# Quantised attention: row maxima over two PSUM banks in one instruction, the tile's shift right behind them

## The reference, cut to what matters

```
q = _fq_sym(q, axis=-1); k = _fq_sym(k, axis=-1); v = _fq_sym(v, axis=2)
attn = jnp.einsum('bhqd,bhkd->bhqk', q, k)
attn = jax.nn.softmax(attn.astype(jnp.float32), axis=-1)
attn = _fq_unsigned(attn, axis=-1)      # s = max(row) / 255; round(x / s) clipped to 0..255, times s
out = jnp.einsum('bhqk,bhkd->bhqd', attn, v)
```

## Time and profile before

| what | value |
|---|---|
| median of 3 runs | 3547.64 us (3543.55 to 3548.8) |
| the profiled execution, its time | 3543.03 us |
| its span in the trace | 3541.3 us |
| the changed stage in it | about 938 to 1848 us |
| PE, DVE, ACT busy, share of the span | 77%, 73%, 52% |

### The profile page before, as it was taken

How to read it: one execution, slowest core, us unless ns; L and a number is a source line. 1 busy time by engine, 2 the same in 40 slices (tenths; PEclk the granted TensorE clock), 3 DMA queues, 4 the chain that set the end, 5 groups by cost and what they waited for, 6 DMA issues and landing times. The chain is left out here.

```text
span 3541.3 us, 63656 instructions
## 1 busy us (share of the span) xinstructions
PE 2737.0 (77%) x21394; PEld 1415.9 (40%) x21394; DVE 2572.9 (73%) x4720; ACT 1835.0 (52%) x2658; POOL 701.9 (20%) x577
## 2 busy tenths in 40 slices
PE   5925999785799999999986677786797547758983
PEld 3413444333365656565653333333111223224541
DVE  5555667566799999999984666524797787986547
ACT  2334433232499999999982433313676022434551
POOL 4422000012110101010104233203012503550012
PEclk8966999896899999999998788897998769978996
DMA  4251431200000000000001100100431000023301
GB/s 171 73 202 48 143 119 48 92 0 15 18 13 7 13 7 13 7 13 13 1 12 51 36 0 0 60 15 12 96 72 45 28 20 1 0 65 64 64 7 51
DMA packets 65283, 151.89 MB, mean 43 GB/s; under 512 B 11792, under 2 KB 20000, under 8 KB 63328
## 3 DMA queue, kind: packets, MB, share of 16 engines
q1 hardware_dynamic: 62320, 140.43, 13.1%
q0 software_dynamic: 2800, 9.18, 0.9%
HBM read 93.61 MB, written 24.38 MB: 33 GB/s over the span
## 5 line engine op out<-in xcount | busy, mean ns | idle before, releaser
L1507 DVE TENSOR_REDUCE s_top<-ps 128x1 f32<-128x512 f32 x1024 | 657.8, 685 | 32.8 <-PE ps L1402 32.3
L1476 ACT ACTIVATE s_prob<-ps,s_shift,m_sq 128x1024 int16<-128x1024 f32 x512 | 615.1, 1202 | 31.2 <-DVE s_shift L1515 31.2
L1402 PE MATMUL ps<-s_ks,s_qs 128*128 128x512 f16 x1024 | 352.4, 386 | 61.4 <-issue 15.3
L1407 PEld LDWEIGHTS ps<-ident,s_prob 128*128 128x128 f16 x4096 | 273.2, 98 | 123.3 <-DVE m_o L1525 52.1
L1407 PE MATMUL ps<-ident,s_prob 128*128 128x128 f16 x4096 | 314.6, 220 | 0.7 <-ACT s_prob L1476 0.5
L1395 PE MATMUL ps<-s_ks,s_qs 128*128 128x512 f16 x1024 | 307.2, 382 | 1.1 <-ACT s_prob L1476 0.5
L1482 ACT ACTIVATE s_probT<-ps 128x1024 f16<-128x1024 int16 x256 | 262.1, 1024 | 6.6 <-PE ps L1407 6.4
L246 PE MATMUL ps<-ident,s_parts 128*128 128x128 f16 x768 | 90.9, 291 | 165.9 <-POOL s_parts L237 164.2
L1520 DVE CAST s_probT<-ps 128x1024 f16<-128x1024 int16 x256 | 174.6, 682 | 3.0 <-PE ps L1407 2.9
L2166 DVE TENSOR_SCALAR s_prob<-ps,s_cap 128x1024 f32<-128x1024 f32 x128 | 158.2, 1271 | 25.2 <-PE ps L2075 25.2
L2747 DVE TENSOR_REDUCE s_ntop<-ps 128x1 f32<-128x512 f32 (+3 forms) x256 | 107.5, 484 | 86.6 <-PE ps L2607 86.6
(11 more groups left out here) (379 smaller groups left out, 5990.6 us busy)
## 6 DMA issues: line engine op xcount, KB each, us to landing
s_qs<-m_qT SPq DMA_DIRECT2D x144, 128.0 KB, 2.5
s_ks<-m_kT SPq DMA_DIRECT2D x96, 128.0 KB, 2.4
numbers<-s_numbers SPq DMA_DIRECT2D x21, 512.0 KB, 2.8
s_slabs<-numbers SPq DMA_DIRECT2D x21, 512.0 KB, 3.8
m_ks<-context_parts SPq DMA_DIRECT2D x12, 512.0 KB, 7.5
expert_rows<-s_y SPq DMA_DIRECT2D x19, 256.0 KB, 2.0
s_rows_in<-in_ctx SPq DMA_DIRECT2D x16, 256.0 KB, 3.0
x_sb<-in_x SPq DMA_DIRECT2D x1, 4096.0 KB, 14.2
```

Of the source, the lines that this page charges most:

```text
L1402: pe.matmul(quarter_at(q), qs[:, hb, bass.ds(t * P, P)], ks[:, hb, cols(q, 512)], start=True, stop=True).then_inc(s.top_scored, 1)
L1407: j = pe.transpose(turned(half, F16)[:, cols(m, P)], prob[:, u, cols(8 * half + m, P)].bitcast(F16), k.ident[:])
L1476: act.activation(prob[:, u, cols(half, HALF)], pair(half).rearrange("p m n -> p (m n)"), ACT.Exp, bias=shift[:, u:u + 1], scale=sq[:, bass ...
L1507: dve.tensor_reduce(top4[:, u, q:q + 1], quarter_at(q), AX.X, ALU.max).then_inc(s.top_read, 1)
```

## The change

Banks 4 and 5 become one buffer. PE waits once per half tile, until DVE has read the half before, and fills both banks with two matmuls, of which only the second one counts up `top_scored`. DVE takes the maximum of both banks, 1024 elements, in one reduce: two for a tile in place of four. The two results stand in `top2`. Behind the second one DVE waits for its result, takes the larger of the two (`ntop`), waits for that too, and makes the tile's shift at once, for tile n+2 where it was for tile n+1. Of DVE's steps for a tile `top_of` is gone as a separate step, and the rest keeps its order.

```diff
-            def score_for_top(n, quarters, hb, t):
-                for q in quarters:
-                    pe.wait_ge(s.top_read, 4 * n + q + 1)
-                    pe.matmul(quarter_at(q), qs[:, hb, bass.ds(t * P, P)], ks[:, hb, cols(q, 512)],
-                              start=True, stop=True).then_inc(s.top_scored, 1)
+            def score_for_top(n, half, hb, t):
+                pe.wait_ge(s.top_read, 2 * n + half + 1)
+                for m in range(2):
+                    j = pe.matmul(tops_at[:, m, :], qs[:, hb, bass.ds(t * P, P)], ks[:, hb, cols(2 * half + m, 512)],
+                                  start=True, stop=True)
+                j.then_inc(s.top_scored, 1)
...
-            def tops(n, u, quarters):
-                for q in quarters:
-                    dve.wait_ge(s.top_scored, 4 * n + q + 1)
-                    dve.tensor_reduce(top4[:, u, q:q + 1], quarter_at(q), AX.X, ALU.max).then_inc(s.top_read, 1)
-
-            def top_of(n, u):
-                dve.wait_ge(s.top_read, 4 * n + 4 + 2)
-                v.later(dve.tensor_reduce(ntop[:], top4[:, u, :], AX.X, ALU.max, negate=True))
+            def tops(n, u, half):
+                dve.wait_ge(s.top_scored, 2 * n + half + 1)
+                dve.tensor_reduce(top2[:, u, half:half + 1], tops_at.rearrange("p m n -> p (m n)"), AX.X, ALU.max
+                                  ).then_inc(s.top_read, 1)
 
             def shift_of(n, u):
-                v.catch_up()
+                dve.wait_ge(s.top_read, 2 * n + 3)
+                v.done(dve.tensor_reduce(ntop[:], top2[:, u, :], AX.X, ALU.max, negate=True))
                 dve.tensor_scalar(shift[:, u:u + 1], ntop[:], sq[:, bass.ds(n, 1)], LN255, ALU.mult,
                                   ALU.add).then_inc(s.shift_ready, 1)
...
                 if more:
-                    top_of(n + 1, (u + 1) % R)
-                if more == 2:
-                    tops(n + 2, (u + 2) % R, (0, 1))
-                if more:
-                    shift_of(n + 1, (u + 1) % R)
+                    tops(n + 2, (u + 2) % R, 0)
                 copy(n, u)
                 if not first:
                     evacuate(n - 1)
-                if more == 2:
-                    tops(n + 2, (u + 2) % R, (2, 3))
+                if more:
+                    tops(n + 2, (u + 2) % R, 1)
+                    shift_of(n + 2, (u + 2) % R)
```

More of the change, by code:

```diff
@@ L1335, in attention_quantised @@
         hv = s.sb("hv", [P, R, T, HD], F16)
-        top4 = s.sb("top4", [P, R, 4], F32)
+        top2 = s.sb("top2", [P, R, 2], F32)
         ntop = s.sb("ntop", [P, 1], F32)
@@ L1345, in pair @@
             return k.ps[:, 2 * half:2 * half + 2, :]
-        def quarter_at(q):
-            return k.ps[:, 4 + q % 2, :]
+        tops_at = k.ps[:, 4:6, :]
         def turned(half, dt):
@@ L1421, in tile @@
                 if next2 is not None:
-                    score_for_top(n + 2, (0, 1), *next2)
+                    score_for_top(n + 2, 0, *next2)
                 pe.wait_ge(s.exp_ready, 2 * n + 1)
@@ L1430, in tile @@
                 if next2 is not None:
-                    score_for_top(n + 2, (2, 3), *next2)
+                    score_for_top(n + 2, 1, *next2)
                 pe.wait_ge(s.exp_ready, 2 * n + 2)
@@ L1459, in _ @@
             pe.wait_ge(s.values_ready, 1)
-            score_for_top(0, range(4), 0, 0)
+            score_for_top(0, 0, 0, 0)
+            score_for_top(0, 1, 0, 0)
             score(0, 0, 0)
             score(1, 0, 0)
-            score_for_top(1, range(4), 0, 1)
+            score_for_top(1, 0, 0, 1)
+            score_for_top(1, 1, 0, 1)
             tile(0, 0, (0, 1), (0, 2))
@@ L1526, in evacuate, with tile @@
                                 output.unsqueeze(1)).then_inc(s.evacuated, 1)
-            def tile(n, u, first=False, more=2):
+            def tile(n, u, first=False, more=True):
                 if more:
-                    top_of(n + 1, (u + 1) % R)
-                if more == 2:
-                    tops(n + 2, (u + 2) % R, (0, 1))
-                if more:
-                    shift_of(n + 1, (u + 1) % R)
+                    tops(n + 2, (u + 2) % R, 0)
                 copy(n, u)
@@ L1538, in tile @@
                     evacuate(n - 1)
-                if more == 2:
-                    tops(n + 2, (u + 2) % R, (2, 3))
+                if more:
+                    tops(n + 2, (u + 2) % R, 1)
+                    shift_of(n + 2, (u + 2) % R)
             dve.nop().then_inc(s.half0_copied, 1)
             dve.nop().then_inc(s.evacuated, 1)
[L1544 to L1548, removed]
+            dve.nop().then_inc(s.top_read, 1)
+            for n in range(2):
+                tops(n, n, 0)
+                tops(n, n, 1)
+                shift_of(n, n)
             tile(0, 0, first=True)
@@ L1553, in _ @@
                     tile(2 * R * i + a + 2, (a + 2) % R)
-            tile(NT - 2, (NT - 2) % R, more=1)
-            tile(NT - 1, (NT - 1) % R, more=0)
+            tile(NT - 2, (NT - 2) % R, more=False)
+            tile(NT - 1, (NT - 1) % R, more=False)
             evacuate(NT - 1)
```

## The result

The changed kernel takes 3666.6 us (median of 4 runs, 3663.9 to 3671.86), the kernel before 3548.14 (4 runs, 3543.55 to 3548.8): a ratio of 1.034, 95% interval 1.0325 to 1.0355. It is 118 us slower.

The account below looks back on a forecast made before the run. DVE was taken to bound the kernel at 3.45 us a tile; two reduces of 1.22 us plus refills of 0.70 and 0.775 give 3.915, so 118 us more over 254 tiles: 3665 us, range 3635 to 3715.

Parts of the forecast that it names:

- a closed chain of two reduces and two refills: DVE and PE on banks 4 and 5: reduce, refill, reduce, refill without overlap set the tile at 3.915 us; 81 in 100.
- The bigger reduce: On DVE: a 1024-element reduce lasts 1.22 us and holds DVE 1.135, removing 0.13 us a tile.
- The refill: Between DVE's reduces: PE's wake-up, two matmuls and DVE's wake-up take 0.70 us, or 0.80 with a register-row wait.
- The prediction's list of signs: What the changed profile would show, including tiles of 3.83 us outside PE's inner loop and 3.93 inside.
- The shift is hidden: Behind a tile's second reduce: small reduce and shift take 0.35 to 0.47 us, shorter than the refill beside them.
- The sum: Per tile: two reduces and two refills make 3.915 us, 0.465 over 3.45; over 254 tiles 118 us more.
- PE stands ready: At each refill PE waits for DVE, with 0.14 us to spare at the second pair and 0.53 at the first.
- The rival of a late PE: At the second pair: PE 0.1 us late makes the tile 4.02 us, the kernel about 3690; 8 in 100.
- The rival of a falling clock: On PE: idle gaps lower the granted clock; one tile in four at the lower level gives 3779 us; 7 in 100.
- The refill hidden: On DVE: its own starts decide, at 3.40 to 3.52 us a tile, 3535 to 3565 us; 4 in 100.
- DVE waited 262 times: In the stage: DVE would wait for PE's scores some 250 times, where it waited 9 times.
- DVE's own work: On DVE: two bigger reduces take 2.27 us in place of 2.40, 0.13 us a tile less, 34 us in 254.

Follow-up runs that it names:

- e1: The changed kernel with its two-bank reduces kept and the shift put back where it was before: 3671.8 us, ratio 1.0366 to the kernel before.
- e2: The kernel before, with its four reduces, and only the shift moved right behind the last reduce: 3602.4 us against 3542.3, ratio 1.0175.
- e3: The changed kernel with PE scoring only the first of the two banks, one matmul per refill: 3594.4 us, ratio 1.0152 to the kernel before.
- e5: The kernel before with the small reduce moved behind the next tile's first bank reduce: 3522.1 us against 3544.0, ratio 0.9944.
- e7: The kernel of e2 with DVE's loop written out over 12 tiles in place of 6: 3593.3 us, ratio 1.014 to the kernel before.
- e6: The kernel of e2 with DVE's loop written out over 18 tiles in place of 6: 3628.5 us, ratio 1.0248 to the kernel before.

## Why the prediction was right

It gave 3665 us (3635 to 3715) and 118 us more; measured were 3666.6 and 118. The mechanism came as forecast, a closed chain of two reduces and two refills. That the number is right to 2 us is in part luck: between the two traces the stage grew by some 127 us, of which 5.5 lie ahead of the first copy, a stretch that the sum left at nothing; the runs of either kernel spread over 5 to 8 us.

- **The bigger reduce**, between rows 1.22 us: it is 1.225 (512 of them). It holds DVE for 1.14 until the next start, where 1.135 was worked out.
- **The refill**, 0.70 and 0.80 us from single links of the trace before: 0.71 and 0.80. That PE's wait in a register row makes the difference shows in the tiles: 3.95 inside PE's inner loop and 3.85 outside it. (The prediction's list of signs has 3.93 and 3.83; its own terms add up to 3.94 and 3.84.)
- **The shift is hidden**: e1 takes it away and wins nothing; e2 puts it where no refill hides it, and it costs 0.17 us a tile. It started 0.135 us behind the end of the small reduce, near the upper end of what was given.
- **The sum**: 3.915 us a tile was predicted, and 0.465 over before; the stage grew by 121.5 us in 255 distances, 0.477 each. The small excess, 3 us, is about what the rounds of DVE's loop cost: their tiles of 4.00 us are 0.05 over the others inside PE's inner loop and 0.15 over those outside it. The prediction had that in its upper end alone.
- **PE stands ready** at both pairs: its rows show 0.55 us of waiting ahead of the first and a start 0.07 us behind the reduce's end at the second. The rival of a late PE did not come.
- **The clock** stayed at 1.00 between the boundaries of groups of heads, with PE idle 0.55 us in each tile. The rival of a falling clock did not come. The page "TensorE: Matmul & The Clock Gate" of the Trainium skill, section "A second HAM failure mode: psum-queue depth-cycling", tells of a kernel whose short gaps between groups of matmuls did make the clock go down and up. No run here shows that for gaps of this length.
- **The refill hidden** was the rival of the other sign. e3 shows how far off it was: even with half a refill's matmuls the tile is 3.63, over the 3.45 of before.
- DVE waited 262 times (some 250 predicted), busy 89.37 of 100 (about 89).
- **DVE's own work** did get shorter, as forecast: 2 x 1.14 in place of 4 x 0.60 us, 0.12 a tile (0.13 predicted). With the buffer that the bigger reduces need, each tile still takes 0.48 us more. The page "Perfetto Trace Analysis" of the Trainium skill, section "Optimizing Scalar/DVE Operations", holds that larger operations can improve throughput if the engine is saturated. Here the engine was saturated and the measurement decides: the kernel is 3.4% slower. The fixed cost that this page of the Trainium skill states, and by which the prediction had an estimate of 0.25 us a tile, is about twice what these rows show.

## What to carry to other kernels

Where one engine fills and another empties the same banks, count buffers ahead of instructions: with two buffers of one bank DVE waited for the filling 9 times in the whole stage, with one buffer of two banks the tile became a closed chain of two reduces and two refills, each end of which is another engine's wake-up. Price such a chain link by link from the trace (end to load, load to matmul, matmul to next, end to start); each reduce and each refill came out within about 0.01 us of the sum's terms. What the bigger reduce gives where it keeps two buffers (four banks) no run here shows; all 8 banks are in use. And of the steps around it ask which ones wait for the result of the instruction in front of them: moving one of those by one place (e5) gave 22 us, with all the instructions still there.

## What the runs showed of the hardware beyond that

- A wait that stands in a register row ahead of PE's weight load lets the load start 0.16 us behind the reduce's end (1403.25 to 1403.41), one in the load itself 0.06: 0.1 us a tile for the form of a wait.
- A round of DVE's loop costs nothing in the kernel before, and 0.40 us a tile where the shift's wait for DVE's own result stands at the loop's end (e2 in 36 tiles, e7 in 16).
- With 18 tiles in DVE's loop each round stops DVE for some 3 us, with instruction packets loaded (e6: 114 packets, 37.5 us of issue waits in 13 places); with 12 tiles there is no such stop (e7: 49 packets, no issue wait over 0.3 us ahead of a reduce).
